# Query-key weight and vectors issued from ScalarE's queue, their first use ahead of the first norm

## What is computed

```python
x_norm = _layer_norm(x, ln1_w, ln1_b)
Q = jax.nn.elu(_linear(x_norm, q_w, q_b)) + 1.0
K = jax.nn.elu(_linear(x_norm, k_w, k_b)) + 1.0
V = _linear(x_norm, v_w, v_b)
attn = _causal_linear_attn(Q, K, V)
x = x + _linear(attn, o_w, o_b)
h = jax.nn.gelu(_linear(_layer_norm(x, ln2_w, ln2_b), f1_w, f1_b), approximate=False)
x = x + _linear(h, f2_w, f2_b)
...
h = jnp.einsum('btd,hd->bth', x, absmean(W_fc))
h = layernorm(jax.nn.gelu(h, approximate=False), ln_w, ln_b)
return jnp.einsum('bth,dh->btd', h, absmean(W_proj))
...
x = x + _L0_attn_ref(_layernorm(x), ...)
x = x + _L0_ffn_ref(_layernorm(x), W_fc, ln_w, ln_b, W_proj)
```

## Time and profile before

| | us |
|---|---|
| median of 3 runs (lowest, highest) | 459.2 (458.97, 460.24) |
| the profiled execution's own time | 459.38 |
| its span | 457.6 |
| busy: PE, VectorE (DVE), ScalarE (ACT), POOL | 441.3, 372.4, 323.0, 187.1 |

### The profile page before, as it was taken

How to read it: one execution, slowest core, us unless ns; L and a number is a source line. 1 busy time by engine, 2 the same in 40 slices (tenths; PEclk the granted TensorE clock), 3 DMA queues, 4 the chain that set the end, 5 groups by cost and what they waited for, 6 DMA issues and landing times.

```text
span 457.6 us, 8944 instructions
## 1 busy us (share of the span) xinstructions
PE 441.3 (96%) x2990; PEld 399.6 (87%) x2990; DVE 372.4 (81%) x1212; ACT 323.0 (71%) x604; POOL 187.1 (41%) x188
## 2 busy tenths in 40 slices
PE   3898999999999999999999999999999999999997
PEld 3786897999989899889989999889998899888977
DVE  6899888867898679986798778987799778876776
ACT  4896856997379854998469963898469885686163
POOL 3887042543247043540537041560536323370333
PEclk9999999999999999999999999999999999999999
DMA  8333000000010002000020002000020000000001
GB/s 237 120 106 127 0 2 1 1 25 1 24 46 25 2 0 70 2 23 1 2 69 2 24 1 69 2 25 1 0 71 2 23 1 9 17 1 23 1 24 47
DMA packets 10061, 14.09 MB, mean 31 GB/s; under 512 B 800, under 2 KB 9120, under 8 KB 9504
## 3 DMA queue, kind: packets, MB, share of 16 engines
q1 hardware_dynamic: 10016, 13.52, 8.9%
HBM read 9.32 MB, written 4.19 MB: 30 GB/s over the span
## 4 chain that ended last, share of the span: by engine, by line
PE 83%; issue 5%; DVE 4%; POOL 2%; DMA 2%; ACT 1%; SPq 1%; POOLq 0%; ACTq 0%
PE bank_f L425 13%; PE bank_p L473 11%; PE bank_y L208 6%; PE bank_y L209 6%; PE bank_y L439 6%; PE bank_y L210 6%; PE bank_f L208 5%; PE bank_f L209 5%; PE bank_f L210 5%; PE bank_a L208 4%; PE bank_a L210 4%; PE bank_a L209 4%; PE bank_a L216 2%; DMA x_odd<-in_x 2%; PE bank_f L216 2%
## 5 line engine op out<-in xcount | busy, mean ns | idle before, releaser
L1188 POOL TENSOR_TENSOR rs<-ve,neg_half 128x2 f32<-128x2 f32 x48 | 33.7, 702 | 204.0 <-DVE ve L872 196.6
L208 PE MATMUL bank_y<-wf_hi,h_hi 128*128 128x256 f32 x240 | 67.2, 280 | 0.0
L209 PE MATMUL bank_y<-wf_lo,h_hi 128*128 128x256 f32 x240 | 67.1, 280 | 0.0
L210 PE MATMUL bank_y<-wf_hi,h_lo 128*128 128x256 f32 x240 | 67.1, 279 | 0.0
L933 DVE TENSOR_TENSOR h_lo<-bank_f,h_hi 128x512 fp32r<-128x512 f32 x60 | 41.2, 686 | 27.5 <-ACT h_hi L686 27.4
L473 PE MATMUL bank_p<-wpj_t,g_hi 128*128 128x256 f32 x240 | 60.6, 288 | 0.0
L678 ACT ACTIVATE bank_f<-bank_f,f_bias 128x512 f32<-128x512 f32 x64 | 42.3, 661 | 25.4 <-PE bank_f L210 24.9
L1068 DVE SCALAR_TENSOR_TENSOR g_lo<-bank_y,vec,g_hi 128x256 fp32r<-128x256 f32 x128 | 55.0, 476 | 4.5 <-ACT g_hi L715 4.1
L473 PE MATMUL bank_p<-wpj_t,g_lo 128*128 128x256 f32 x240 | 58.6, 280 | 0.0
L715 ACT ACTIVATE g_hi<-bank_y,vec 128x256 fp32r<-128x256 f32 x128 | 53.5, 477 | 7.2 <-PE bank_y L439 3.8
L425 PE MATMUL bank_f<-wfc_t,z3T_hi 128*128 128x512 f32 x128 | 53.7, 420 | 0.8 <-DVE z3T_lo L933 0.8
(11 more groups left out here) (292 smaller groups left out, 1206.1 us busy)
## 6 DMA issues: line engine op xcount, KB each, us to landing
out<-y_yc SPq DMA_DIRECT2D x15, 256.0 KB, 2.2
x_even<-in_x SPq DMA_DIRECT2D x8, 256.0 KB, 2.9
x_odd<-in_x SPq DMA_DIRECT2D x8, 256.0 KB, 3.0
h<-in_f SPq DMA_DIRECT2D x1, 1024.0 KB, 8.0
y_yc<-in_f SPq DMA_DIRECT2D x1, 1024.0 KB, 10.4
h<-in_fc SPq DMA_DIRECT2D x1, 1024.0 KB, 4.7
h<-in_pj SPq DMA_DIRECT2D x1, 1024.0 KB, 4.9
z<-in_wv SPq DMA_DIRECT2D x1, 256.0 KB, 4.0
```

What stands on the lines that cost most here:

```text
L208: pe.matmul(ps, w[0], r[0], start=start, stop=False, skip_group_check=skip)
L209: pe.matmul(ps, w[0], r[1], start=False, stop=False, skip_group_check=skip)
L210: return pe.matmul(ps, w[1], r[0], start=False, stop=stop, skip_group_check=skip)
L1188: pool.tensor_tensor(rs[n][:, 2 * h:2 * h + 2], ve[n][:, 2 * h:2 * h + 2], neg_half[:, 0:2], ALU.pow).then_inc(s[f"ln{n + 1}_rs"], 1)
```

## The change

The loads of wqk and vec are issued by ScalarE, as its first two instructions, in place of SP. On ScalarE wqk_hi() and ln3_hi() stand ahead of u_norm(0, 0) and u_norm(0, 1) in place of behind them. Every other instruction stands where it stood, and the semaphores are the same.

```diff
@@ -180,8 +180,6 @@
             load_x(0)
-            sp.dma_start(wqk_raw, wqk_d).then_inc(s["wqk_loaded"], 16)
-            sp.dma_start(vec[:], vec_d).then_inc(s["vec_loaded"], 16)
             sp.dma_start(wv_raw, wv_d).then_inc(s["wv_loaded"], 16)
             sp.dma_start(wo_raw, wo_d).then_inc(s["wo_loaded"], 16)
@@ -524,6 +522,10 @@
         @block.scalar
         def _(act):
+            def load_first_weights():
+                act.dma_start(wqk_raw, wqk_d).then_inc(s["wqk_loaded"], 16)
+                act.dma_start(vec[:], vec_d).then_inc(s["vec_loaded"], 16)
+
             def tables():
@@ -717,7 +719,7 @@
             def first():
 
-                tables(); u_norm(0, 0); u_norm(0, 1); wqk_hi(); ln3_hi(); u_hi(0, 0); u_hi(0, 1); wf1_hi(0)
+                load_first_weights(); tables(); wqk_hi(); ln3_hi(); u_norm(0, 0); u_norm(0, 1); u_hi(0, 0); u_hi(0, 1); wf1_hi(0)
```

## The result

The changed kernel takes 460.36 us in the median of 22 runs (459.38 to 461.29), the kernel before 459.69 in as many beside it. The ratio is 1.0014, with a 95% interval of 1.0007 to 1.0020: slower by 0.67 us, far inside the 0.3% that count as no change, but a real loss, and above the upper end of the predicted range. Of the 1.06 us between 460.36 and the forecast, 0.49 were in the base: the forecast started from a median of 459.20 over three runs, which over 22 is 459.69. One of those 22 runs of the kernel before took 490.19 us; it counts as slow and is not in the ratio.

The account below looks back on a forecast made before the run. The start, until TensorE gets into its stride, was taken to bound the kernel: x_odd 0.5 us sooner, x_even 0.4 us later, so qk_max 0.12 us later; 459.2 + 0.1 = 459.3 us, range 458.5 to 460.2.

Parts of the forecast that it names:

- The hole in the DMA share: From 3.75 to 5.25 us the DMA share was 0.65, 0.52 us idle; SP's larger loads, issued sooner, should fill it.
- s: How much sooner x_odd lands with two issues fewer on SP: taken as 0.5 us, bounds zero and 0.98.
- Rival 3: On ScalarE the table load stays ahead of the two issues; x_even undisturbed, 458.9 us, at worst 459.3; chance 0.05.
- Rival 1: At the start x_even is not disturbed, x_odd lands 0.3 us or more earlier: full gain, 458.9 us; chance 0.25.
- rival 2: Sharing DMA engines costs x_even more, or weight or vec lands after 6.5 us: slower, up to 459.7 us; chance 0.12.
- the case that was given 0.89: Whole kernel's time the same, not to be told from no change (about 0.3%, 1.4 us): chance 0.89.
- d: Delay of x_even's first half by the loads beside it, moving qk_mm's end equally: taken as 0.4 us, bounds zero and 0.75.
- the weight at slightly under full rate: Ground for the 0.4 us delay of x_even: the weight's 131 KB take 0.35 us at 380 GB/s.
- a second half with slack: vec starts half a microsecond later and meets x_even's second half, which lands at 4.3 and is read after 4.91.
- 0.28 us, and no more: qk_max starts at 14.21 behind x_odd's statistics, could start at 13.93: cap of any gain on the load side.
- the end of qk_mm at 13.91: Last matmul of qk_mm(0) on TensorE ends at 13.52 + 0.39 = 13.91 us, letting qk_max start at 13.93.
- The sum: qk_max starts at the later of 14.21 - s and 13.93 + d: 14.33, 0.12 us later; the end moves equally.

Follow-up runs that it names:

- the two orders of VectorE: Kernel before with only VectorE's order changed: qk_max(0) ahead of x_odd's first statistics, 461.0 us, ratio 1.0031; both statistics halves ahead of qk_max(0), 461.07 us, ratio 1.0034.
- The 18 added calls: 18 matmuls of mean_w, result unread, put ahead of qkb on TensorE: kernel before 459.74 us, ratio 1.0007; changed kernel 458.64, ratio 0.9982, repeated 458.65, ratio 0.9980.
- the issue during the table load: Both loads on ScalarE, written behind tables() but issued while the table load ran, old order of norms, against the kernel before: 460.16 us, ratio 1.0016.
- both statistics first: Changed kernel with 18 matmuls ahead of qkb and both halves of x_odd's statistics ahead of qk_max(0) on VectorE: 461.1 us, ratio 1.0026 to before.
- 26 calls: Kernel before with 26 matmuls of mean_w, result unread, put ahead of qkb on TensorE: 459.74 us, ratio 1.0007.

## Why the prediction was wrong in its range and right in most steps

**Right.** The stretch that decides is the start, and nothing after 60 us has moved. The hole in the DMA share fills. x_odd comes sooner: its gain s, taken as 0.5 us, is 0.55 by the first two profiles and 0.6 by the medians. No cost of ScalarE's order shows: the order alone is at 1.0002, and the two steps end 1.15 us before the norm's input is there. Rival 3 (the table load first) is out by the row of the issue at 0.80. Rival 1 (x_even undisturbed) is out by the reading at 4.73. What came is rival 2, x_even's delay dearer than x_odd's gain, and the direction had only 0.12. The ratio lies within 0.3%, the case that was given 0.89.

**Wrong, first: the size of d.** I took 0.4 us, and 0.75 for its upper bound. In the profiled execution it was 4.73 - 3.65 = 1.08. Over the seven profiles in which ScalarE issues both loads at the start, x_even is read at 4.22 to 4.73, median 4.28; over the eight with both on SP behind it, at 3.48 to 3.70, median 3.58. So the usual d is 0.7, and 0.5 to 1.2 occur. The step that failed was "the weight at slightly under full rate". The weight alone cost 0.76 in its one profile. The prediction had the better rate in its own rows: the 197 GB/s at which weight and vectors moved before give 0.67 us for the weight's 131 KB and 0.76 for both. It read that row and then took a value near the full rate's 0.35. After the change the engines moved 279 GB/s from 2.5 to 3.5 us, 251 in the second profile and 318 with the loads alone, and not 380: with the weight beside x_even the full rate isn't there. That the vectors meet a second half with slack did hold, as far as is shown: the second half is read without a wait, and both loads delay x_even by 0.7 in the median, no more than the weight alone. Why the small loads move so slowly is not shown. The Trainium skill, "DMA: Bandwidth & Descriptors", section "Queues, rings and completion order", has the engines take turns by packets. That 17.5 KB alone cost 0.36 us is in accord with it, but no run here shows the turns, and the weight, with the same 144 packets, cost twice as much. With both loads ahead in one queue, x_even at 4.50, no turns are needed: it is issued 0.9 us later.

**Wrong, second: the load of x_odd costs the kernel "0.28 us, and no more", and the end of qk_mm at 13.91 to which d is added.** Both were read off one execution. The row with 2.78 us for wvo_mm is one draw: in the five profiles with the loads untouched and no matmul added (before twice, the order of ScalarE alone, and the two orders of VectorE) it is 2.78, 3.10 and three times 3.62. Where it is 3.62, TensorE is done at 14.9 to 15.0 and stands behind x_odd by itself, so that there is no gain of 0.28 to set against d, and d should be paid in full. Where it is 2.78 or 3.10, x_odd stands last and there are 0.3 to 0.5 us to win. In the changed kernel TensorE stands last in all three profiles (the change's two and the loads alone), by 1.0 to 2.4 us: qk_relu at 15.20 to 16.25, against x_odd's readings of 12.62 to 12.93 and their 1.26 us. The sum should thus have been d less some tenths, 0.3 to 0.7 us, and that is what the ratios of 1.0014, 1.0014 and 1.0007 say, 0.3 to 0.7 us. (Between single variants the times don't follow x_even's reading so closely: with the weight alone it is 0.76 us late and the ratio is 1.0003, at most 1.0012; there x_odd is issued 0.5 us sooner.) The further 1.22 us by which qk_mm's end moved in the first profile are nearly all the draw: in the order alone, with x_even undisturbed, the same 3.62 puts that end at 14.57 + 0.39 = 14.96, already 1.05 later than in the earlier trace rows. Nor does a late x_even bring the slow pace with it: with the weight alone on ScalarE x_even is read at 4.34 and wvo_mm takes 2.51. From wvo_mm's start to the end of qk_mm it is 4.18 to 5.39 us in the five untouched profiles and 3.86 to 5.39 in the four with both loads on ScalarE at the start and no matmul added. So the change isn't seen to bring the slow pace; whether it draws it more often, so few profiles can't say.

**Wrong, third: the base.** The forecast was tied to three runs with a median of 459.20. The 22 beside the change gave 459.69, and in other sessions medians of 21 to 33 runs lay from 459.38 to 459.83. The range's upper end, 460.2, left 1.0 us above the base. About half of that was used up before the change did anything.

**The gain.** The cap of 0.28 us was right for the one execution it was read from, but it is no cap of the gain: once TensorE isn't last, the earlier x_odd pays more. The 18 added calls bring nothing or at most about 0.2 us in the kernel before (1.0007; 459.30 for 459.53 without the runs at the lower clock) and 0.18 to 0.20% in the changed one (0.9982 and 0.9980), about 0.9 us; what limits the kernel before at that point is x_odd, read at 13.29 behind a wait of 2.16 us.

**Open.** Why the issue during the table load loses as much as the whole change with x_even read only 0.3 us late; where and why the granted clock falls in some executions, in nine of 12 of the changed kernel with 18 calls and both statistics first; and what makes TensorE's first matmuls fast or slow in an execution of unchanged code. For the last, the runs show only that work ahead of them makes them fast.

## What to carry to other kernels

A load issued on a second queue beside the first load that matters can delay that one, and by more than its bytes at the full rate say: here 17.5 KB by about 0.36 us and 128 KB by about 0.76. Take the rate from a stretch in which the small loads themselves move, and set the delay against the strand that hangs on the first load. Where two strands end within half a microsecond of each other, one profile's slack between them is no cap: profile the same kernel several times, and look for the event that keeps its distance from the end, since that one tells which strand decides. A gain on the strand that isn't last isn't lost, but has to be paired with one on the other: the quicker TensorE alone brought next to nothing here, the loads alone a small loss, and both together a gain of 0.2%. Before a median is explained, sort its runs by their mean granted clock.

## What the runs showed of the hardware

- TensorE's rate at the start isn't in the granted clock. One and the same matmul went 7 times per us and then 12 times, with 1.00 in both rows, and wvo_mm took 1.89, 2.78, 3.10 or 3.62 us with 1.00 throughout. With 18 or 26 calls ahead of it it was 1.89 each time.
- ScalarE's sequencer sends out a DMA while a table load is running: the issue at 0.98 lies within the load from 0.80 to 2.08 and needs 0.38 us.
- In one profile 17.5 KB on a second queue went with a reading of the 256 KB load about 0.36 us later than usual (3.94 for 3.48 to 3.70), and 128 KB with one 0.76 us later (4.34); each load was 144 packets. The same 17.5 KB, issued at 2.75 us behind another queue's large loads, took 6.0 us to land, in place of 3.8 ahead of them.
- Some runs of one and the same kernel have a lower mean granted clock, and they are longer. Of the 142 runs of the kernel before that stand beside the experiments, 14 had 0.995 or 0.996 and took 460.39 to 461.58 us; the 128 others had 0.999 or 1.000 and took 458.65 to 460.44.
